# Fused attention and feed-forward stage of a two-layer gated model: row norms and rounding on ScalarE, a new TensorE order, two tiles' keys and values ahead of the loop, two drain tiles per step

## What is computed

```python
x = x + tanh(g_xattn[0]) * L0_xattn(layernorm(x), ctx)      # 16 heads of 8
x = x + tanh(g_ffn[0])   * L0_ffn(layernorm(x))             # 8 experts, 2 chosen per row
x = x + tanh(g_xattn[1]) * L1_xattn(layernorm(x), ctx)      # 16 heads of 64
x = x + tanh(g_ffn[1])   * L1_ffn(layernorm(x))

def L1_xattn(q, kv):
    f = (q @ w_q) . (kv @ w_k) / 8 + mask                   # per head
    return softmax(f) @ (kv @ w_v) @ out_w.T + out_b

def act_quant(x):
    scale = 127 / clip(max(|x|, rows), 1e-5)
    return clip(round(x * scale), -128, 127) / scale

def L1_ffn(x):                                              # weights rounded to -1, 0, 1 times a scale
    h = act_quant(x) @ w1q.T                                # 128 -> 512
    h = silu(conv3(h) + conv_b)                             # three taps along the 64 rows, each channel alone
    return act_quant(h) @ w2q.T                             # 512 -> 128
```

## Time and profile before

| | us |
|---|---|
| median of 3 runs | 1706.23 (1705.69 to 1706.85) |
| the profiled execution | 1699.43 |
| its span | 1697.8 |
| fused stage, first instruction of its VectorE to the end | 750.46 to 1697.8 |

### The profile page before, as it was taken

How to read it: one execution, slowest core, us unless ns; L and a number is a source line. 1 busy time by engine, 2 the same in 40 slices (tenths; PEclk the granted TensorE clock), 3 DMA queues, 4 the chain that set the end, 5 groups by cost and what they waited for, 6 DMA issues and landing times.

```text
span 1697.8 us, 50196 instructions
## 1 busy us (share of the span) xinstructions
PE 1530.3 (90%) x20035; PEld 1196.4 (70%) x20035; DVE 1183.3 (70%) x2972; ACT 973.6 (57%) x1855; POOL 694.6 (41%) x573
## 2 busy tenths in 40 slices
PE   5999999996499999958999999999999999999965
PEld 3777777775277777746787777877777777787743
DVE  5788888898121221227789888888888888877775
ACT  3878787872233333314566666666666666666644
POOL 2335666777200000025765544445544444333300
PEclk9999999996699999978999999999999999999986
DMA  9999950011344445411100000000000000000000
GB/s 282 403 387 380 373 192 25 29 33 41 113 143 158 140 150 158 144 60 28 33 28 18 18 23 21 21 21 21 22 22 21 21 21 15 12 12 15 7 8 18
DMA packets 86884, 154.25 MB, mean 91 GB/s; under 512 B 10448, under 2 KB 33104, under 8 KB 86416
## 3 DMA queue, kind: packets, MB, share of 16 engines
q1 hardware_dynamic: 74352, 123.85, 21.8%
q0 software_dynamic: 11312, 27.02, 4.8%
q10 hardware_dynamic: 1008, 0.40, 0.1%
HBM read 57.64 MB, written 93.59 MB: 89 GB/s over the span
## 4 chain that ended last, share of the span: by engine, by line
PE 25%; DVE 12%; issue 9%; ACT 8%; POOL 1%; DMA 0%; ACTq 0%; DVEq 0%; POOLq 0%
PE L1psM L1171 7%; PE L1psY L1122 3%; PE L1psY L1129 3%; PE L1psY L1114 3%; ACT L1PT L1284 2%; DVE L1am L1530 2%; PE L1psS L1140 2%; PE L1psT L1163 2%; ACT L1hc L1301 2%; DVE L1hs L1525 1%; PE L1psF L1188 1%; PE L1psF L1196 1%; PE L1psT L1149 1%; ACT L1OT L1289 1%; ACT L1KT L1263 1%
## 5 line engine op out<-in xcount | busy, mean ns | idle before, releaser
L1601 POOL TENSOR_TENSOR L1sc<-L1sc,L1rden 128x1024 f32<-128x1024 f32 x64 | 138.9, 2170 | 283.0 <-DVE L1rden L1492 282.9
L911 ACT ACTIVATE GhT<-GpsH,Gwx 128x512 f32<-128x512 f32 x156 | 107.2, 687 | 187.9 <-PE GpsH L887 187.4
L927 DVE TENSOR_TENSOR Gyg<-GpsY,Gwx 128x512 f32<-128x512 f32 x39 | 27.0, 692 | 228.0 <-PE GpsY L894 228.0
L788 POOL TENSOR_TENSOR L0sc<-L0sc,L0top 128x1024 f32<-128x1024 f32 x64 | 121.6, 1900 | 149.4 <-DVE L0top L546 149.3
L1596 POOL TENSOR_TENSOR L1sc<-L1sc,L1top 128x1024 f32<-128x1024 f32 x64 | 121.9, 1904 | 131.1 <-DVE L1top L1483 131.0
L1313 ACT ACTIVATE L1z<-L1psF,L1nround,L1scl 128x512 f32<-128x512 f32 x51 | 39.7, 778 | 234.4 <-DVE L1scl L1538 234.4
L894 PEld LDWEIGHTS GpsY<-Gwx,GhT 128*128 128x128 f32 x1248 | 145.2, 192 | 17.7 <-issue 17.7
L1171 PE MATMUL L1psM<-L1WO,L1OT 128*128 128x128 f32 x1024 | 129.5, 280 | 31.2 <-DVE X L1544 31.1
L1122 PEld LDWEIGHTS L1psY<-L1xnT,L1WQ 128*128 128x128 f32 x1024 | 129.1, 193 | 30.8 <-ACT L1xnT L1258 17.2
L1114 PE MATMUL L1psY<-L1cx,L1WK 128*128 128x128 f32 x1024 | 137.3, 278 | 10.4 <-DMA L1cx<-in_ctxT 10.4
L894 PE MATMUL GpsY<-Gwx,GhT 128*128 128x128 f32 x1248 | 145.6, 275 | 0.0
(11 more groups left out here) (248 smaller groups left out, 3741.7 us busy)
## 6 DMA issues: line engine op xcount, KB each, us to landing
rows_in<-L0zero SPq DMA_DIRECT2D x1, 34560.0 KB, 95.6
rows_out<-L0zero SPq DMA_DIRECT2D x1, 34560.0 KB, 196.3
Gwx<-in_experts SPq DMA_DIRECT2D x39, 579.0 KB, 4.2
Gxg<-rows_in SPq DMA_DIRECT2D x39, 256.0 KB, 4.3
rows_out<-Gyg POOLq DMA_DIRECT2D x39, 256.0 KB, 4.3
L1cx<-in_ctxT SPq DMA_DIRECT2D x64, 64.0 KB, 1.8
out<-X SPq DMA_DIRECT2D x64, 64.0 KB, 1.7
L0ctxT<-in_ctxT SPq DMA_DIRECT2D x1, 2560.0 KB, 19.3
```

What stands on the lines that cost most here:

```text
L788: nc.gpsimd.tensor_tensor(sc[:, t % 4, :, :], sc[:, t % 4, :, :], top[:, t % 2, :].unsqueeze(2).broadcast_to([P, H, S]), ALU.subtract).the ...
L911: nc.scalar.activation(hT[:, u, m, :], psH[:, m, :], ACT.Gelu, bias=wx[:, w, ob1 + m:ob1 + m + 1]).then_inc(s["h_ready"], 1)
L1601: nc.gpsimd.tensor_tensor(sc[:, t % SR, :, :], sc[:, t % SR, :, :], broad(rden[:, t % 2, :]), ALU.mult).then_inc(s["probs_ready"], 1)
```

## The change

Row norms: the list of moments has an 18th operation, minus mean times inverse deviation (`nmr1`, `nmr2`), and the norm of the attention's rows is an ACTIVATE on ScalarE with that as bias. It stands at the end of ScalarE's step. The norm ahead of the feed-forward part (`normalise2`) and its rounding (`round2`) are four ACTIVATEs of a tile each on ScalarE; the maximum is now taken of the normed rows, so two small products leave VectorE. `inv2` is made on GpSimd (`unit`). TensorE's order changes inside the step, and VectorE's maximum and scales go between `add_bias` and `tops`. K and V of tiles 0 and 1 are made ahead of the loop, the first norm is of tile 0 alone, and rows are collected by two per step from tile 1 on. In the drain up to two tiles and two `hidden` share a step, with S0, S1 and M or Y1 as further banks; steps end at 75.

The core of the diff:

```diff
-        NORMS = [(0, 2), (2, 4), (4, 6), (6, 8), (8, 12), (12, 16)] + [(i, i + 8) for i in range(16, NT, 8)]
+        NORMS = [(0, 1), (1, 2), (2, 4), (4, 6), (6, 8), (8, 12), (12, 16)] + [(i, i + 8) for i in range(16, NT, 8)]
+        NORM_STEPS = {1: (0, 1), 2: (1, 1), 3: (2, 2), 4: (4, 2)}
-        for t in range(2, NT):
-            k = 0 if t < 4 else max(1 + (t - 4) // 2, t - 13)
-            collects.setdefault(k, []).append(t)
+        for t in range(1, NT):
+            collects.setdefault(max(t // 2, t - 13), []).append(t)
...
-        STEPS = NT + FB
-        NORM_OPS, FFN_OPS = 17, 25
+        NORM_OPS = 18
+        FFN_OPS = [(range(0, 9), 0, 0), (range(9, 18), 1, 0), (range(18, 21), 2, 2), (range(21, 22), 3, 3)]
+        hidden_step = [n + FH for n in range(56)] + [67, 67, 68, 68, 70, 70, 71, 71]
+        turn_step = [t + FT for t in range(52)] + [68, 68, 69, 69, 70, 70, 71, 71, 73, 73, 74, 74]
+        xq_step = [G4 * g + FX for g in range(NG - 1)] + [69]
+        STEPS = 76
...
+            for t in range(2):
+                for c in range(2):
+                    project_k(t, c)
+            for t in range(2):
+                for b in range(2):
+                    project_v(t, b)
             for k in range(STEPS):
...
-                if tx is not None:
-                    project_k(tx, 1)
-                if n is not None:
+                for n in at(hidden_step, k):
                     hidden(n)
                 if tx is not None:
+                    if tx > 1:
+                        project_k(tx, 1)
                     project_q(tx, 0)
                 if tt is not None:
                     values(tt)
+                for t in at(turn_step, k - 1):
+                    turn_back(t)
                 if tx is not None:
                     project_q(tx, 1)
...
+            def layernorm(t):
+                act.wait_ge(s["norm1_ready"], chunk(t) + 1)
+                wait(act, s["xnT_ps"], t - 1)
+                nc.scalar.activation(xn[:, t % 2, :], X[:, t, :], ACT.Identity, bias=nmr1[:, t:t + 1],
+                                     scale=rstd1[:, t:t + 1]).then_inc(s["xn_ready"], 1)
+
+            def normalise2(g):
+                act.wait_ge(s["norm2_ready"], g + 1)
+                wait(act, s["xq_ready"], g - 1)
+                for j in range(G4):
+                    t = G4 * g + j
+                    last = nc.scalar.activation(xd[:, g % 2, j, :], X[:, t, :], ACT.Identity, bias=nmr2[:, t:t + 1],
+                                                scale=rstd2[:, t:t + 1])
+                last.then_inc(s["xd_ready"], 1)
+
+            def round2(g):
+                act.wait_ge(s["xs_ready"], g + 1)
+                act.wait_ge(s["xd_ready"], g + 1)
+                for j in range(G4):
+                    t = G4 * g + j
+                    last = nc.scalar.activation(xd[:, g % 2, j, :], xd[:, g % 2, j, :], ACT.Identity, bias=nround[:, 0:1],
+                                                scale=scl[:, t:t + 1])
+                last.then_inc(s["y_ready"], 1)
...
-                elif i == 17:
-                    ins = vec.tensor_tensor(x, X[:, at, :], wide(mean2[:, at], G4), ALU.subtract)
...
-                if tile(k, LN) is not None:
-                    layernorm(k)
...
                 if tx is not None:
                     add_bias(tx)
+                for t in at(turn_step, k):
+                    largest(t)
+                    scales(t)
+                if tx is not None:
                     tops(tx)
                 if tt is not None:
                     add_x(tt)
...
+            def unit(t):
+
+                pool.wait_ge(s["step_ready"], t + 1)
+                nc.gpsimd.tensor_tensor(inv2[:, t:t + 1], step2[:, t:t + 1], half[:], ALU.mult).then_inc(s["inv_ready"], 1)
```

## The result

The changed kernel takes **1750.5 us** (median of 4 runs, 1748.4 to 1756.2) against 1706.5 (1705.7 to 1708.7) for the kernel before: a ratio of 1.0258, 95% interval 1.0242 to 1.0275. It is slower by 44 us; 24 were forecast, in a range of 1698 to 1752.

What follows compares the result with a forecast made beforehand. It took a loop over TensorE, VectorE and ScalarE (13.17 us plus VectorE lateness) to bound the kernel. Steady steps +42, start -6, ramp -3, drain -9 gave +24 us on 1706.23: 1730 us, range 1698 to 1752.

Steps and rivals of the forecast that it cites:

- the ends of the stage: Start, ramp and drain of the fused stage, outside the 48 steady steps: -6, -3 and -9 us, -18 together.
- The waits: New TensorE waits: `turn_back` 1.1 us for the convolution, `turn_x` 0.3 for `add_x`, `turn_h` 0.9 every fourth step.
- the loop: Path over TensorE, VectorE and ScalarE from scores to the next scores: 14.15 us forecast, against 13.17 before.
- Steady steps: The 48 repeating steps of the fused stage: 14.5 us each, 696 us against 654, +42 us.
- The four passes: `normalise2` and `round2` on ScalarE in two of four steps: 0.35 us each, 0.1 a step on average.
- The step with `turn_xq`: Every fourth step, where `turn_h` waits for ScalarE's copy of bank F: +1.0 us, or 0.25 a step.
- Start: From stage start to first scores, K and V of tiles 0 and 1 filling TensorE's wait: -6 us (0 to -10).
- Ramp: The six steps before the steady ones, where VectorE loses about 0.5 us a step: -3 us (0 to -6).
- rival A: VectorE was the limit and its relief counts: steps fall to TensorE's 12.9 us, 1653 us in all; chance 0.14.
- Drain: The last steps, 14 before and nine after: 67.4 us falls to 58.5, -9 us (-5 to -13).
- B: The ends win: steps at 14.1 us (+23), start, ramp and drain at their best (-29), 1700 us; chance 0.10.
- C: TensorE's clock falls to 1.2 GHz in one step of ten because of the waits: 1791 us; chance 0.04.

Runs made afterwards that it cites:

- centre-first: The changed kernel with `centre` ahead of the copy of K half 1 on ScalarE, nothing else moved: 1716.8 us, ratio 1.0068 to the kernel before.
- the old order: The changed kernel with all engines' lists inside the loop ordered as before, moved work, start and drain kept: 1727.7 us, ratio 1.0125 to the kernel before.
- the kernel with all three moves: The changed kernel with `centre` first, `turn_xq` ahead of the scores and the four ScalarE passes at the end of the step before: 1688.2 us, 1792.7 on the slower chip.
- the four kernels run there: On the slower chip: changed kernel with `turn_back` behind Q half 1 (1800.7 us); with `centre` first plus passes moved (1787.6), `turn_xq` moved (1793.9) or both (1792.7).

## Why the prediction was right, and where it was off

The direction and the mechanism came out as forecast. The size came out only just: 1750.5 us is 1.5 us inside the range's upper end. That end, +46, was drawn with the ends of the stage still winning; the prediction's own bounds (+61 for the steps, 0, 0 and -5 for start, ramp and drain) reach +56. The step was 0.13 short and everything outside the steady steps won 2 us in place of 18, and both misses went the same way; that their sum stayed inside is in part luck.

**The waits** that were named are in the trace. In the plain step (S + ...): `turn_x` 5.0 forecast, 4.92 measured; K half 1's copy 7.5 and 7.44; `centre` 8.0 and 7.94; `turn_back` 10.5 and 10.41, after a wait of 1.1, measured 1.02 for the row and 1.15 over all; from there to the scores 3.65 and 3.80; the loop 14.15 and 14.21. That centre-first shortened the step by as much as it brought `turn_back` forward shows that this chain sets it. `turn_x`'s wait for `add_x` was forecast at 0.3 a step. The list names `add_x` in two steps only, but has the weight load ahead of `turn_x` standing 10.3 us in 36 pieces, 0.29 each, under "issue":

```profile
PEld L1psM L1124 <- issue: 10.3, 36, 0.9
```

The timeline shows that it is this wait. In the steps without `turn_xq`, from K half 0 (1127.26) to `turn_x` (1128.81) it is 1.55 us, in place of 1.33 before, and `turn_x` starts 0.15 after the end of `add_x` (1128.38 + 0.28) in each of them. In the steps with `turn_xq` it is 1.33 again and `add_x` is 0.51 earlier. So the wait is 0.22 in three of four steps.

One reading of the kernel before was loose, and did no harm. The prediction closed the loop of before through the convolution and `turn_back`. In that stretch the list of waits has none for `turn_back`: it started 0.27 us after the end of the convolution in most steps, where 0.15 is the least, and 30.1 of the 30.5 us in which TensorE was idle were `project_out` waiting for `residual`. There are steps of 12.94 us beside the walked 13.17. So the wait for `residual` held TensorE (in 29 of the 48 steps) and the convolution missed doing so by 0.12 us; the new order takes the first out of the way and adds Q half 1 to the second.

**Steady steps: +42 forecast, +48.2 measured.** The missing 0.13 a step has three parts. The plain loop, 0.06: `turn_back` came 0.09 earlier than walked, and from there to the scores it is 0.15 longer, since V in two halves around `project` takes 2.02 us in place of 1.87 (1029.24 to 1031.11 before). The four passes, 0.35 each forecast, are 0.41 in a row:

```profile
1100.24 1.64 ACT L1303 ACTIVATE L1xd<-L1xd,L1nround,L1scl 128x128 f32<-128x128 f32 x4
```

and their steps took 14.47 and 14.46, 0.26 over the plain one in place of 0.2: 0.03 a step. The step with `turn_xq` took 15.37, 1.16 over the plain one in place of 1.0: 0.04.

**What the passes cost** was called 0.1 a step. Against the order of this kernel that is nearly right (0.13), because the wait for K half 1 covered them. It is not what they cost in general: 0.64 a step in the old order (its steps with passes average 14.81 us, the others 13.53; the rest of the moved work wins 0.13 there), 0.42 once `centre` is first. The prediction priced an edit beside a wait that another edit had made. In the sum this does no harm, but it would have misled whoever repaired the order and expected the passes to stay free.

**The ends.** Start: -6 forecast, -2.0 measured, and the prefill's share is nil. Ramp, the six steps: -3 forecast, +1.7 measured, and +4.5 with the seven steps ahead of them (82.30 against 79.49). The ramp's term held that VectorE's relief counts while VectorE looks full, the idea of rival A, and it was wrong there too: TensorE was fuller (72.28 of 75.10 us, VectorE 70.24) and VectorE got only 0.4 us less to do. From the first `add_x` to the end of the ramp V's products now wait 6.1 us in 14 pieces for ScalarE's copy of Q, 3.3 in 4 before; why the rest was lost stays open. Drain: -9 forecast, "near 58"; measured 60.42, -7, of which the two tiles a step are -10.7. With the two next steps, 24.58 against 22.27, the parts give +48.2 - 2.0 + 4.5 + 2.3 - 7.0 = +46.

**The rivals.** A (VectorE was the limit) is ruled out by the kernel in the old order. The Trainium skill's rule for it ("Perfetto Trace Analysis", "Identifying the Most-Contended Engine": work on the engine with the highest occupancy first, where TensorE is judged by its weight loads, here 77%, and not by its 95% of matmul time) would have led astray here: VectorE was 85% busy, and its relief by 40 us, with the work moved to ScalarE, came with +20 us. B did not occur: the steady steps cost 48 and not 23 us, and all the rest won 2 and not 29. C did not occur: the granted clock is 1.00 through 48 waits of 1.15 us.

## What to carry to other kernels

When several engines each run a list written by hand, a step's length is the longest closed path through all of them, so walk that path for the changed order before counting busy time: here the relief of VectorE, 85% busy, was worth 0.13 us a step in the old order at best and an exchange of two neighbours on an engine that is busy 70% of the time was worth 33 us. If one list is reordered, go through the lists that consume its results and put them in the same order (`hidden` ahead of K half 1 asks for `centre` ahead of K half 1's copy); and put moved work where its engine stands idle for something late, not where it stands behind something early. An edit that looks free may be free only beside another edit's wait.

## What the hardware showed besides

**Two VectorE instructions take more than twice their time behind a pass of GpSimd.** The groups of `twice_silu` (L1585) and of the first instruction of `collect` (L1439) in the changed kernel:

```profile
L1585 DVE SCALAR_TENSOR_TENSOR L1hs<-L1hs,L1hc 128x512 f32<-128x512 f32 x48 | 76.5, 1594 | 43.1 <-ACT L1hs L1360 43.0
...
L1439 DVE SCALAR_TENSOR_TENSOR L1x<-L1yr,weight,X 128x128 f32<-128x128 f32 x35 | 59.0, 1685 | 0.0
```

and the same two in the kernel with the old order, where they start at another moment of GpSimd's passes:

```profile
L1589 DVE SCALAR_TENSOR_TENSOR L1hs<-L1hs,L1hc 128x512 f32<-128x512 f32 x50 | 33.6, 671 | 1.1
...
L1443 DVE SCALAR_TENSOR_TENSOR L1x<-L1yr,weight,X 128x128 f32<-128x128 f32 x35 | 25.8, 738 | 0.0
```

These are 1594 against 671 ns and 1685 against 738, together 77 us of the steady stretch, and an order sets it. It is why VectorE's busy time fell by 8 us in place of 40. In the kernel with the old order small norm instructions take part of it back, since they now start inside a pass (the added operation of the moments, L1468, takes 1863 ns, and 251 in the changed kernel). It didn't set the end here. The Trainium skill, "SBUF — State Buffer", "SBUF: two separate sides", says that a VectorE instruction with two SBUF inputs and a GpSimd instruction share a pair of ports, that the one that starts first has it for its whole length, and that the other one blocks. The rows agree: one `twice_silu` of the changed kernel starts at 1092.96 beside the pass `normalise` of 1092.20 to 1094.10 and ends at 1094.65, 0.55 after the pass, so it did its work behind it.

```profile
1092.20 1.90 POOL L1660 TENSOR_TENSOR L1sc<-L1sc,L1rden 128x1024 f32<-128x1024 f32 x1 [3.40 <-DVE L1rden L1552]
```

```profile
1092.96 1.69 DVE L1585 SCALAR_TENSOR_TENSOR L1hs<-L1hs,L1hc 128x512 f32<-128x512 f32 x1 [0.84 <-ACT L1hs L1360]
```

All of them but one start 0.67 to 0.94 us into a pass and end 2.45 after its start, whenever they began. In the kernel with the old order `twice_silu` starts 0.01 to 0.17 us ahead of the pass in each step, takes 0.63 to 0.69, and it is the pass that is longer, 2.21 to 2.44 in place of 1.90:

```profile
1086.46 0.66 DVE L1589 SCALAR_TENSOR_TENSOR L1hs<-L1hs,L1hc 128x512 f32<-128x512 f32 x1
1086.62 2.26 POOL L1664 TENSOR_TENSOR L1sc<-L1sc,L1rden 128x1024 f32<-128x1024 f32 x1 [5.45 <-DVE L1rden L1556]
```

**On one chip TensorE stood without a releaser.** On the chip where the kernel before took 73 us more, and the kernel with all three moves 104 (1792.7 against 1688.2), TensorE stood inside the 64 small products of `values`, with no wait for another engine in the profile ("issue"). That its instructions came late is a reading of this, not shown. The groups of that line over the loop, there and on another chip, of the same kernel:

```profile
L1182 PE MATMUL L1psT<-L1PT,L1V 64*64 64x64 f32 x2176 | 57.7, 225 | 13.8 <-issue 13.8
```

```profile
L1182 PE MATMUL L1psT<-L1PT,L1V 64*64 64x64 f32 x2304 | 42.0, 221 | 0.0
```

The 13.8 us are a part of it: the profile of this kernel is 83 us longer there, 21 ahead of the fused stage, 38 up to `add_x` of tile 12 and 23 in the 48 steps. Early steps took up to 17.96 us there in place of 11.37, and from tile 13 on every step up to about 1490 us took 14.05 or more whatever the order; then it ended, when GpSimd's gathers of rows end too (1486.91, and the last such stand of TensorE at 1488.38). That the two are connected was not tried and stays open, as does why this chip alone showed it. It hides differences of order: the four kernels run there took 1788 to 1801 us, within 0.8% of one another, although their undisturbed steps differ by 6% (53.17 against 56.60 for four).
